# Attention scores in two 64-row tiles of TensorE's array, a pair of head groups at a time

## The reference, cut to what matters

```python
q = split(einsum(x_norm, wq) + bq) * SCALE        # 16 heads of 16 features
k = split(einsum(ctx, wk) + bk);  v = split(einsum(ctx, wv) + bv)
scores = einsum('bhnrd,bhncd->bhnrc', qb, kc)     # contraction over 16 features of a head
attn = softmax(where(valid, scores, neg_inf))
x = x + tanh(g_xattn) * (attn @ v @ wo + bo)
x = x + tanh(g_ffn) * experts(layernorm(x))       # 8 experts, the best 2 of each token
```

## Time and profile before

| | us |
|---|---|
| median of 3 runs (range) | 544.91 (544.62 to 545.47) |
| the profiled execution, whole | 546.27 |
| its span, first to last instruction | 544.40 |
| mean granted TensorE clock, share of full | 0.961 |
| TensorE matmuls busy | 486.3 |
| VectorE busy | 361.0 |
| ScalarE busy | 298.3 |
| GpSimd busy | 210.0 |

### The profile page before, as it was taken

The page is one execution under the profiler, slowest core; times in us unless marked ns, Lnnn a source line. Parts: engine busy times, 40 slices in busy tenths (PEclk is TensorE's granted clock), DMA queues, the critical chain, the costliest instruction groups (busy, mean ns, idle before and its releaser), DMA issues.

```text
span 544.4 us, 10775 instructions
## 1 busy us (share of the span) xinstructions
PE 486.3 (89%) x3553; PEld 449.7 (83%) x3553; DVE 361.0 (66%) x878; ACT 298.3 (55%) x756; POOL 210.0 (39%) x271
## 2 busy tenths in 40 slices
PE   5799999899989877359899899999999999999991
PEld 4688887777778666249799899999999999999991
DVE  6757878988797988827758285376753767644340
ACT  3679877787868653317546273274732646433140
POOL 9535776787778556420030303203031030301212
PEclk9899999999999987759999899999999999999997
DMA  8859322314132611173545536146470454101011
GB/s 273 210 102 262 78 40 71 79 49 80 45 74 66 199 50 52 36 242 138 203 82 183 130 88 175 16 132 186 127 183 10 137 173 139 21 11 19 11 20 20
DMA packets 41651, 57.34 MB, mean 105 GB/s; under 512 B 3722, under 2 KB 38577, under 8 KB 39553
## 3 DMA queue, kind: packets, MB, share of 16 engines
q1 hardware_dynamic: 35168, 48.62, 30.8%
q0 software_dynamic: 6144, 8.07, 8.8%
q10 hardware_dynamic: 288, 0.00, 0.0%
HBM read 36.24 MB, written 16.72 MB: 97 GB/s over the span
## 4 chain that ended last, share of the span: by engine, by line
PE 54%; DVE 2%; issue 2%; POOL 1%; DMA 1%; ACT 0%; POOLq 0%; DVEq 0%
PE bank L1420 17%; PE bank L1422 17%; PE bank L1421 17%; PE bank L1414 2%; PE bank L1343 1%; POOL expert_rows L479 1%; DMA expert_rows<-xr,slotu 1%; PE bank L1286 0%; POOL out_tokens L535 0%; DVE bXl L1086 0%; DVE ysc L1123 0%; DVE hL L1113 0%; PE bank L1220 0%; POOL lnr L452 0%; DVE topi L854 0%
## 5 line engine op out<-in xcount | busy, mean ns | idle before, releaser
L535 POOL DMA_INDIRECT out_tokens<-ysc,rows x32 | 49.3, 1542 | 251.2 <-DVE ysc L1123 245.9
L1420 PE MATMUL bank<-bXh,wh 128*128 128x384 f32 (+1 forms) x384 | 122.7, 319 | 2.8 <-issue 2.5
L1422 PE MATMUL bank<-bXh,wl 128*128 128x384 f32 (+1 forms) x384 | 122.5, 319 | 0.0
L1421 PE MATMUL bank<-bXl,wh 128*128 128x384 f32 (+1 forms) x384 | 122.3, 319 | 0.0
L739 ACT ACTIVATE sil<-bank 128x384 f32<-128x384 f32 (+1 forms) x96 | 43.7, 456 | 129.3 <-PE bank L1422 129.2
L1109 DVE TENSOR_TENSOR hF<-sil,bank 128x384 f32<-128x384 f32 (+1 forms) x96 | 48.9, 510 | 77.9 <-ACT sil L739 71.2
L622 ACT ACTIVATE p<-bank,nm 128x128 f32<-128x128 f32 x256 | 73.6, 387 | 17.1 <-DVE nm L909 17.1
L1420 PEld LDWEIGHTS bank<-bXh,wh 128*128 128x128 f32 x384 | 73.2, 191 | 3.2 <-issue 3.2
L1420 PE MATMUL bank<-wh,hH 128*128 128x256 f32 x256 | 73.8, 288 | 0.3 <-DVE ysc L1123 0.3
L1421 PEld LDWEIGHTS bank<-bXl,wh 128*128 128x128 f32 x384 | 73.2, 191 | 0.0
L1422 PEld LDWEIGHTS bank<-bXh,wl 128*128 128x128 f32 x384 | 73.1, 190 | 0.0
(11 more groups left out here) (147 smaller groups left out, 886.4 us busy)
## 6 DMA issues: line engine op xcount, KB each, us to landing
stage<-in_w12T SPq DMA_DIRECT2D x16, 1024.0 KB
stage<-in_w3T SPq DMA_DIRECT2D x8, 1024.0 KB
expert_rows<-padrow SPq DMA_DIRECT2D x8, 662.5 KB, 7.9
rows<-expert_rows SPq DMA_DIRECT2D x7, 662.5 KB, 4.3
kM<-k SPq DMA_DIRECT2D x64, 64.0 KB, 2.4
cT<-in_ctxT SPq DMA_DIRECT2D x8, 256.0 KB, 3.3
out_tokens<-x_all SPq DMA_DIRECT2D x8, 256.0 KB, 2.4
x_all<-in_x SPq DMA_DIRECT2D x2, 640.0 KB, 8.2
```

Of the source, the lines that this page charges most:

```text
L535: pool.indirect_dma_start(out=out, out_offset=bass.IndirectOffsetOnAxis(rows[par][:, c, D + E:ROW].bitcast(U32), 0), in_=ysc[par][:, c, :] ...
L1420: nc.tensor.matmul(out_ap, ah, bh, start=start, stop=False)
L1421: nc.tensor.matmul(out_ap, ah, bl, start=False, stop=False)
L1422: return nc.tensor.matmul(out_ap, al, bh, start=False, stop=stop)
```

## The change

Scores are now computed for two groups at once, in even steps only. Both mask matmuls come first, into S[0] and S[1]. Then each of the three products is issued for the even group on rows 0 to 63 and for the odd group on rows 64 to 127, alternating, each into its own bank. The wait is now for `act_exp` to be G: both groups of the pair before must have their exponentials. `largest` and `exps` go in pairs in the even steps, `prob_columns` too. The orders around them are rewritten: on TensorE `project_out` and `logits` move to steps 2, 4 and 6, on ScalarE all copies move to odd steps, and in step 5 the order is now `queries`, `output_columns`, `exps_of_logits`, which was `exps_of_logits`, `output_columns`, `queries` in step 4. VectorE's `sum_exps` stays at the front of step 5.

```diff
@@ ScalarE, body
-                    if g == 0 and prev1:
+                    if cur and g % 2 == 0:
+                        exps(G, 0, not prev1 and g < 2)
+                        exps(G + 1, 1, not prev1 and g < 2)
+                    if g == 1 and nxt:
+                        input_columns(n + 1)
+                    if g == 1 and prev1:
                         output_columns(SB * (n - 1), Xo)
+                    if g == 1 and prev1 and cur:
+                        values2(n, par)
+                    if g == 3 and nxt:
+                        keys(n + 1, Xp, True)
+                    if g == 3 and prev2:
+                        x2_columns(n - 2, Xo)
+                    if g == 5 and nxt:
+                        queries(n + 1, 1 - par, Xp, True)
+                    if g == 5 and prev1:
+                        output_columns(SB * (n - 1) + 1, Xo)
+                    if g == 5 and prev2:
+                        exps_of_logits(n - 2)
                     if g == 7 and nxt:
                         values(n + 1, Xp)
...
                         values1(n + 1, 1 - par)
-                    if g == 4 and prev2:
-                        exps_of_logits(n - 2)
-                    if g == 4 and prev1:
-                        output_columns(SB * (n - 1) + 1, Xo)
-                    if g == 4 and nxt:
-                        queries(n + 1, 1 - par, Xp, True)
...
@@ VectorE, body
+                    if cur and g % 2 == 0:
+                        largest(G, 0)
+                        largest(G + 1, 1)
                     if g in (2, 6) and prev1:
                         gated(n - 1, 1 - par, g // 4, Xo)
...
-                    if cur:
-                        largest(G, g)
@@ TensorE, scores
-                if g < 2:
-                    pe.wait_ge(ld_km[g], KM * (n + 1))
+                    pe.wait_ge(ld_km[0], KM * (n + 1))
+                    pe.wait_ge(ld_km[1], KM * (n + 1))
                 if not early:
-                    pe.wait_ge(act_exp, G - 1)
-                nc.tensor.matmul(S[g % 2][:, :], identb[:, :], causal[:, :, :], start=True, stop=False)
+                    pe.wait_ge(act_exp, G)
+                for h in range(2):
+                    nc.tensor.matmul(S[h][:, :], identb[:, :], causal[:, :, :], start=True, stop=False)
 
                 for sq, sk in ((0, 0), (0, 1), (1, 0)):
-                    ins = nc.tensor.matmul(S[g % 2][:, :], q2[par][:, sq, hq // 2, b * T:(b + 1) * T],
-                                           kM[par][:, sk, GH * hq:GH * hq + GH, b * T:(b + 1) * T],
-                                           start=False, stop=(sq == 1))
-                ins.then_inc(pe_s, 1)
+                    for h in range(2):
+                        r = slice(h * P // 2, (h + 1) * P // 2)
+                        first = GH * (hq + h)
+                        ins = nc.tensor.matmul(S[h][:, :], q2[par][r, sq, hq // 2, b * T:(b + 1) * T],
+                                               kM[par][r, sk, first:first + GH, b * T:(b + 1) * T],
+                                               start=False, stop=(sq == 1))
+                        if sq == 1:
+                            ins.then_inc(pe_s, 1)
@@ TensorE, body
-                    if cur:
+                    if cur and g % 2 == 0:
                         scores(G, g, n, par, not prev1 and g < 2)
                     if g == 7 and prev2:
                         pe.wait_ge(dve_x2, SB * n)
                         ranks(n - 2, Xo)
-                    if (cur and g >= 2) or (prev1 and g < 2):
-                        prob_columns(G - 2, g % 2, not prev1 and g < 4)
+                    if g % 2 == 0 and ((cur and g >= 2) or (prev1 and g < 2)):
+                        prob_columns(G - 2, 0, not prev1 and g < 4)
+                        prob_columns(G - 1, 1, not prev1 and g < 4)
+                    if g == 2 and prev1:
+                        project_out(SB * (n - 1), Xo)
+                    elif g == 4 and prev2:
+                        logits(n - 2, Xo)
+                    elif g == 6 and prev1:
+                        project_out(SB * (n - 1) + 1, Xo)
...
```

More of the change, by code:

```diff
@@ L635, in body @@
                         high_probs(G - 2, g % 2, not prev1 and g < 4)
-                    if g == 0 and prev1:
-                        output_columns(SB * (n - 1), Xo)
+                    if cur and g % 2 == 0:
[4 more added lines that the diff above has]
+                    if g == 1 and prev1:
+                        output_columns(SB * (n - 1), Xo)
+                    if g == 1 and prev1 and cur:
[10 more added lines that the diff above has]
+                        exps_of_logits(n - 2)
                     if g == 7 and nxt:
                         values(n + 1, Xp)
[L640 to L643, removed]
-                    if cur:
-                        exps(G, g, not prev1 and g < 2)
-                    if g == 7 and nxt:
-                        values1(n + 1, 1 - par)
-                    if g == 4 and prev2:
-                        exps_of_logits(n - 2)
-                    if g == 4 and prev1:
-                        output_columns(SB * (n - 1) + 1, Xo)
-                    if g == 4 and nxt:
-                        queries(n + 1, 1 - par, Xp, True)
[L654 to L657, removed]
+                        values1(n + 1, 1 - par)
             act.wait_ge(ld_g, 16)
@@ L1308, in body @@
                             values(n + 1, 1 - par, Xp)
-                    if g == 1 and prev1:
-                        project_out(SB * (n - 1), Xo)
-                    elif g == 2 and prev2:
+                    if g == 2 and prev2:
                         pe.wait_ge(dve_x2, SB * (n - 1) + 1)
                         x2_columns(n - 2, par, Xo)
-                    elif g == 3 and prev2:
-                        logits(n - 2, Xo)
                     elif g == 4 and prev1:
@@ L1322, in body @@
                         output_columns(SB * (n - 1) + 1, Xo)
-                    elif g == 5 and prev1:
-                        project_out(SB * (n - 1) + 1, Xo)
                     if g == 0 and nxt:
```

## The result

The changed kernel takes 580.37 us, the median of 4 runs (578.74 to 580.48), against 545.19 (544.62 to 546.13) for the kernel before on the same chip: a ratio of 1.064, 95% interval 1.0617 to 1.0664. It is slower by 35 us where 15.6 were forecast. The profiled execution spans 578.5 us at a mean granted clock of 0.925; before, these were 544.4 us and 0.961.

A forecast was written before the change was run, and what follows sets the result against it. TensorE and VectorE were taken to share the bound. Longer bodies 2 to 7 and the tail, less bodies 0 and 1, summed to +12.6 us, giving a 557.5 median; 3 for the clock made 560.5, range 546 to 575.

The forecast's parts named there:

- the clock term: TensorE's half clock after 3 us pauses, slowing transposes and projection ahead of the residual: 3 us taken, 7 if every time.
- the wait at `sum_exps`: Step 5: VectorE stands 2.5 us until ScalarE, queries first, finishes the exponentials of the logits.
- the start: Body 0: its first pair waits for the keys of both halves; no cost priced, body 0 given -0.5 us.
- body 1: Body without routing: four pairs of 4.55, 5.4, 4.6 and 5.2, 19.8 us against 20.54, so -0.8.
- Scores: TensorE's scores of a pair: 1.44 us instead of 1.82, tiles side by side with two switches.
- a switch: TensorE's array going between 128 and 64 rows: one exposed latency each way, 0.15 us.
- Rival B: The two tiles run in turn, a pair costs 0.68 us more: 571 us; over 566, 0.15 together with E.
- D4 to D6: From maxima of step 4 to those of step 6, holding the new wait: 8.8 us, a loss of 2.0.
- D2 to D4: From maxima of step 2 to those of step 4, TensorE the late one: 5.7 us.
- E: Half clock through most bodies also stretches keys and scores of steps 2 and 3: 570 to 576; 0.15 with B.

The follow-up runs named there:

- f2: The changed kernel with the reciprocals of `heads_out` written to spare columns of the output bank in PSUM: 578.56 us.
- e3: The changed kernel with `exps_of_logits` right behind the exponentials of step 4, ahead of `high_probs`, queries and output columns: 561.61 us.
- e4: The changed kernel with 24 idle transposes on TensorE between the two sets of transposes of step 6: 578.61 us.
- e13: e12 with 12 idle transposes on TensorE in step 0 of bodies 3 to 7: 557.08 us.
- g2: f3 with 12 idle transposes in step 0 of bodies 3 to 7, ahead of the output columns: 550.55 us.
- e12: e11 with the even bank's mask written earlier and body 0's even products not waiting for the odd group's keys: 555.10 us.
- e11: e3 with `weigh_values` of even steps moved behind the second `prob_columns`: 560.98 us.
- f3: e12 with the reciprocals of `heads_out` written to spare columns of the output bank in PSUM: 552.56 us.
- f1: The kernel before with the reciprocals of `heads_out` written to spare columns of the output bank in PSUM: 541.83 us.
- g1: f3 with the products of the scores on all 128 rows again: 559.89 us.
- e2: The kernel before, in single steps and its own order, with each group's products on its own 64 rows: 553.98 us.
- e10: The kernel before with only ScalarE's order in step 4 changed to queries, output columns, then `exps_of_logits`: 551.53 us.

## Why the prediction was wrong

The direction and the mechanism were right, the size was not: 580.4 lies above the range. The step that failed is the clock term of the sum, 3 us, where the half clock took 11.7 at least. Three smaller terms failed beside it: the wait at `sum_exps` (2.5 us a body, measured 3.52), the start (put at nothing) and body 1.

Where the profiled execution left the forecast can be read from the maxima. At D0 of body 7 it is 33.7 us later than before (219.15 against 185.41), where the forecast has 12.6 - 0.8 - 0.5 + 3 = 14.3. Of the 19.4 too many, 4.4 arose before body 1, 1.2 in body 1 and 13.9 in bodies 2 to 6.

**Scores.** 1.44 us a pair taken, 1.42 measured; 0.15 a switch taken, 0.28 for two measured. Rival B (tiles in turn) is out.

**The wait at sum_exps.** Forecast 2.5 us, measured 3.52; D4 to D6 9.2 to 10.0, not 8.8, which makes 4.8 us over bodies 2 to 6. Two things make the difference in the fences above: the exponentials started 1.33 after D4, not 0.95, and `high_probs` waited 0.90 for `weigh_values`, which stand behind logits, queries and output columns on TensorE. That second wait is in L628 of the kernel, and I left it out of the schedule. The same wait stands in step 3, in D2 to D4, which took 6.2 to 7.6 us against 5.7, 4.3 more over bodies 2 to 6. ScalarE, TensorE and GpSimd in step 3 of body 5:

```profile
168.16 0.60 ACT L629 ACTIVATE pT<-bank 128x512 f16<-128x512 f32 x1 [1.06 <-PE bank L1278]
168.61 0.38 PE L1278 MATMUL bank<-V,pT 128*128 128x50 bf16 x8 [0.55 <-POOL V L427]
167.38 1.17 POOL L427 TENSOR_TENSOR V<-vf,V 128x512 bf16<-128x512 f32 x1
```

Here `weigh_values` also waits for GpSimd's last third of the values, which ended 9.18 us after D0, not 8.36. The block of `heads_scale` is no large part of it: without the block, in f2, D2 to D4 is 6.3 to 7.7. How the 4.3 divide between these waits and the half clock stays open.

**The clock.** This is the term most undersized: I took 3 us, and all 7 would have been too few. Half clock lengthened D6 to D0 from the 7.44 of e3 and e4 by 7.5 us over bodies 2 to 6 (8.53, 9.54, 8.73, 8.35 and 9.56), and D0 to D2 from 4.47 by 4.2 over bodies 3 to 7. I had priced one pause in a body and only its effect on the residual; there are two, and the second stretches scores and transposes of step 2. The fillers show that these are the clock's: with them D6 to D0 is 7.44 (e4), and D0 to D2 shows no long body (4.27 in e13 and g2). Curing the first pause alone gained 1.8 us of the median (e4).

**The start.** Body 0 was given -0.5. The first pair waits for both halves of the keys and falls into a stretch of half clock, and the first maxima came 4.25 us later (24.35 against 20.10). e12 took 3.5 of it back. I had named the wait and not priced it.

**Body 1** was given -0.8 and came out at +0.4 (20.67 to 21.05): its pairs take 4.85, 5.41, 4.82 and 5.97 us, against 4.55, 5.4, 4.6 and 5.2 in the forecast, with nothing to hide it.

Of the rivals, E (half clock through most bodies, 570 and more) was the nearest; I gave it and B 0.15 together.

Where the 35 us are, by undoing them in one order: `lex` ahead of the queries 18.8, with the pause and the half clock that it brings (e3); `weigh_values` earlier 0.6 (e11); start and mask 5.9 (e12); the port 2.5 (f3). What is left over f1 is 10.7, already less the 7 that the tiles save (g1), and 2.0 of it is half clock (g2). f1 itself lies 3.2 under before: 18.8 + 0.6 + 5.9 + 2.5 + 10.7 - 3.2 = 35.3. These are differences of medians; the ratios give 17.6 + 2.0 + 6.1 + 2.6 + 11.0 - 4.5 = 34.8. In another order the shares would differ. That the remaining 8.7 us are the loop of the pairs is argued, from the distances between maxima, and not shown. From f1 to g2 the first maxima come 0.3 us later, body 0 grows by 1.1, bodies 3 to 6 by 1.2 each and body 7 by 1.5 up to D6. The orders that were rewritten with the pairs (`project_out`, `logits`, ScalarE's copies) are in this rest too, and no run separates them. A run that gives the pairs a second set of banks was not tried, since the kernel's eight are all in use.

## What to carry to other kernels

A faster matmul that needs both of two alternating buffers at once trades overlap for rate; before taking it, write the loop down in order, with every wait of every instruction between two uses of the buffer, those for buffers read by others included. With one set of buffers, a small instruction behind long ones on a third engine cost several times what it cost with two (here 3.1 us a body against 0.7, with a longer wait and some 1.5 us of half clock in the 3.1). And price the clock by pauses, all of them: curing the longest left the loss behind the next.

## What the runs showed of the hardware

Six fp32r matmuls of 64 rows and 512 columns in two tiles, each tile into its own bank, take the time of three (e2 against after: 1.19 and 1.42 with one more mask). Going from 128 rows to 64 and back costs 0.28 us (e2, 1.19 against 0.91).

A VectorE operation with both inputs in SBUF lasted 0.29 us at its shortest and up to 3.29 beside GpSimd's operations on SBUF (e13), and 0.29 in all 32 rows when one input came from PSUM (f1). The Trainium skill (SBUF — State Buffer, section SBUF: two separate sides) says that VectorE and GpSimd take a shared pair of ports as an exclusive lock, not as shared bandwidth, and names VectorE operations with two SBUF inputs against GpSimd operations that read SBUF; the 2.89 us row, which ends as GpSimd's third operation ends, agrees, and adds that the block can span several of its operations.

In the changed kernel the granted clock of TensorE fell to the 1.2 GHz level behind the pause of 3.2 to 3.6 us in each of bodies 2 to 6. Behind the pause of 1.6 to 1.9 us around D0 it fell in bodies 3, 4 and 6 and not in 5; in f3, with 1.88 us in each body, it fell in 3 and 6 and not in 4 and 5. It stayed at 1.00 in bodies 3 to 6 of e10, with one pause of 1.4 us in each, and in bodies 1 to 6 of before, whose longest pause was 1.05. So the length of a pause alone doesn't tell whether it falls.
